# Summing 20 instead of 18 token tiles inside the expert loop, four just behind it, with tables by five stages and earlier first slots

## What is computed

```python
x = x + _L0_attn_ref(_layernorm(x), ...)   # only the first 16 tokens of each batch go through attention, three iterations
x = x + _L0_ffn_ref(_layernorm(x), ...)    # for the others attention adds a bias alone
# _L0_ffn_ref, for each token:
scores = sigmoid(tokens @ router_weight.T)      # 32 experts in 4 groups
topk_idx, topk_w = ...                          # best 2 groups, best 4 experts in them, weights normalised, times 2.5
gate_vals, up_vals = silu(tokens @ gate_w[e].T), tokens @ up_w[e].T
expert_out = (gate_vals * up_vals) @ down_w[e].T
mixed = (expert_out of the 4 chosen experts * topk_w).sum()
return mixed + shared_expert(tokens)            # a dense expert for every token
```

## Time and profile before

| | |
|---|---|
| median of 3 runs | 484.57 us (483.71 to 491.29) |
| profiled execution, its own time | 480.79 us |
| its span, first to last instruction | 478.9 us |
| PE busy | 372.5 us (78%) |
| DVE busy | 300.5 us (63%) |
| POOL busy | 298.0 us (62%) |
| ACT busy | 239.2 us (50%) |
| mean granted clock of PE | 0.927 of full speed |
| DMA | 98.01 MB, 205 GB/s over the span |

### The profile page before, as it was taken

How to read it: one execution, slowest core, us unless ns; L and a number is a source line. 1 busy time by engine, 2 the same in 40 slices (tenths; PEclk the granted TensorE clock), 3 DMA queues, 4 the chain that set the end, 5 groups by cost and what they waited for, 6 DMA issues and landing times.

```text
span 478.9 us, 9278 instructions
## 1 busy us (share of the span) xinstructions
PE 372.5 (78%) x2363; PEld 302.2 (63%) x2363; DVE 300.5 (63%) x1010; ACT 239.2 (50%) x611; POOL 298.0 (62%) x437
## 2 busy tenths in 40 slices
PE   0668989997888673479999999999999788969000
PEld 0544757573455251468899999999999677967000
DVE  3878877759988342147588854444444676858197
ACT  1546755585735552344565665666566444435000
POOL 5410888888888888688776766666666445446100
PEclk9999988999999899589999999999999989889655
DMA  7980123522386387648987755555556887687696
GB/s 173 282 257 2 60 105 108 190 106 111 113 330 235 113 331 258 230 148 272 303 273 230 228 172 157 180 167 174 167 158 208 275 287 220 214 292 225 224 407 200
DMA packets 46457, 98.01 MB, mean 205 GB/s; under 512 B 8633, under 2 KB 30782, under 8 KB 44992
## 3 DMA queue, kind: packets, MB, share of 16 engines
q1 hardware_dynamic: 33392, 62.70, 41.9%
q0 software_dynamic: 12720, 34.62, 19.4%
q10 hardware_dynamic: 288, 0.03, 0.0%
HBM read 53.93 MB, written 44.57 MB: 206 GB/s over the span
## 4 chain that ended last, share of the span: by engine, by line
PE 15%; issue 14%; POOL 13%; DVE 8%; DMA 8%; DVEq 1%; SPq 0%; ACT 0%; POOLq 0%; ACTq 0%
POOL pairs_dram L714 11%; PE two_banks L1127 8%; DVE x_sb L1731 6%; PE two_banks L1140 4%; DMA pairs_dram<-routing,loopb 2%; PE two_banks L1114 2%; DMA routing<-pairs_dram 2%; DMA loopb<-pairs_dram 2%; POOL slots_dram L706 1%; DVE staged_w L1757 1%; DMA gu_w<-pairs_dram 1%; DMA slots_dram<-loopb,slot_i 1%; DVEq L1748 1%; DVE routing L1717 1%; PE two_banks L963 0%
## 5 line engine op out<-in xcount | busy, mean ns | idle before, releaser
L714 POOL DMA_INDIRECT pairs_dram<-routing,loopb x137 | 139.3, 1017 | 85.7 <-issue 60.0
L1127 PE MATMUL two_banks<-routing,staged_w 128*128 128x128 f32 x1096 | 150.7, 282 | 2.7 <-ACT routing L855 1.7
L706 POOL DMA_INDIRECT slots_dram<-loopb,slot_i x128 | 128.1, 1001 | 27.0 <-issue 26.0
L1127 PEld LDWEIGHTS two_banks<-routing,staged_w 128*128 128x128 f32 x1096 | 138.6, 198 | 3.6 <-ACT routing L855 2.1
L1140 PE MATMUL two_banks<-dn_w,routing 128*128 x274 | 85.3, 394 | 15.1 <-DVE routing L1717 15.1
L1717 DVE TENSOR_TENSOR routing<-routing,two_banks 128x128 f32<-128x128 f32 x137 | 38.9, 284 | 76.2 <-ACT routing L860 72.5
L1757 DVE COPY staged_w<-gu_w 128x512 f32 x137 | 65.2, 476 | 16.8 <-issue 8.4
L865 ACT ACTIVATE routing<-two_banks 128x256 f32<-128x256 f32 x137 | 52.5, 383 | 38.3 <-PE two_banks L1140 38.3
L860 ACT ACTIVATE routing<-two_banks 128x128 f32<-128x128 f32 x137 | 37.9, 277 | 66.7 <-PE two_banks L1127 66.5
L954 PE MATMUL two_banks<-gu_w,sgu_w 128*128 128x512 f32 (+1 forms) x128 | 64.7, 639 | 6.8 <-DVE loopb L1513 5.8
L1114 PE MATMUL two_banks<-ident,loopb 128*128 128x128 f32 x274 | 54.3, 282 | 10.8 <-DMA loopb<-slots_dram 10.5
(11 more groups left out here) (278 smaller groups left out, 405.5 us busy)
## 6 DMA issues: line engine op xcount, KB each, us to landing
loopb<-slots_dram SPq DMA_DIRECT2D x137, 128.5 KB, 2.7
gu_w<-pairs_dram SPq DMA_DIRECT2D x14, 512.0 KB, 9.0
routing<-pairs_dram SPq DMA_DIRECT2D x12, 512.0 KB, 4.5
slots_dram<-blank SPq DMA_DIRECT2D x33, 136.0 KB, 28.1
gu_w<-in_gate_up SPq DMA_DIRECT2D x2, 2048.0 KB, 11.1
loopb<-pairs_dram SPq DMA_DIRECT2D x6, 512.0 KB, 3.9
gu_w<-in_gate_up SPq DMA_DIRECT2D x1, 2560.0 KB, 9.5
pairs_dram<-routing,loopb POOLq DMA_INDIRECT x137, 3.4
```

What stands on the lines that cost most here:

```text
L706: pool.indirect_dma_start(out=slots_dram, out_offset=bass.IndirectOffsetOnAxis(ap=slot_i[:, at:at + 1], axis=0), in_=xg[:, r, :] if n < TT ...
L714: pool.indirect_dma_start(out=pairs_dram, out_offset=bass.IndirectOffsetOnAxis(ap=xg[:, place_of(u), D:ROW].bitcast(I32), axis=0), in_=yb[ ...
L1127: ins = pe.matmul(bank[2 + u % 2][:, m * P:(m + 1) * P], staged_w[:, u % 2, c, m * I:(m + 1) * I], xT[:, u % 2, c, :], start=(c == 0), sto ...
```

## The change

Stages are now five, at tiles 8, 16, 20, 24 and 32 (`DONE_BY` 63, 95, 111, 127), in both tables. Twenty tiles are summed in the loop in pairs that start at units 72, 78, 84, 90, 104, 109, 114, 119, 124 and 129, four units each. SP issues the two loads of a pair together, at unit start + 6 of its own order. Four more tiles (q 20 to 23) are loaded when unit 126 has been scattered and summed directly behind the loop; 8 are left for the end. The first group of 8 tiles is stored in SP's unit 110. The first table has 64 entries to work on instead of 32, the second 160 instead of 96. In the first stretch the ranks and slots of tiles 1 to 8 stand earlier on PE and DVE, and the root of tiles 17 to 24 moves on POOL behind the first six indirect DMAs. ACT's program is the same.

```diff
-OUT_GROUPS = [(1, 9), (9, 17), (17, 19), (0, 1), (19, 25), (25, 28), (28, 30), (30, 32)]
-LOADS = TT - 18
+OUT_GROUPS = [(1, 9), (9, 17), (17, 21), (21, 25), (0, 1), (25, 28), (28, 30), (30, 32)]
+LOADS = TT - 24
...
-STAGES = [16, 24, TT]
+STAGES = [8, 16, 20, 24, TT]
 DONE_BY = [(TOPK * P * t + E * (P - 1)) // P for t in STAGES[:-1]]
-IN_LOOP = 18
-SUM_FROM = 101
-SUM_ORDER = [*range(1, IN_LOOP + 1), 0, *range(IN_LOOP + 1, TT)]
+SUM_AT = [72, 78, 84, 90, 104, 109, 114, 119, 124, 129]
+IN_LOOP = 2 * len(SUM_AT)
+BEFORE_END = 24
+SUM_ORDER = [*range(1, BEFORE_END + 1), 0, *range(BEFORE_END + 1, TT)]
 EARLY_LOADS = 5
-assert STAGES[0] == PARTS[1][1] - 1 and DONE_BY[-1] < FIXED and SUM_FROM + IN_LOOP * TOPK // 2 <= FIXED
+LOAD_AT = [at + 6 for at in SUM_AT]
+assert STAGES[:2] == [PARTS[0][1] - 1, PARTS[1][1] - 1] and STAGES[3] == BEFORE_END and DONE_BY[3] < FIXED
+assert all(at - RING + 1 >= DONE_BY[[2 * pair + 2 <= t for t in STAGES].index(True)] for pair, at in enumerate(LOAD_AT))
+assert SUM_AT[-1] + TOPK <= FIXED and LOAD_AT[-1] < FIXED
...
 FILL_PE = [
-    "T0 L0 T1 T2 T3 T4 L1 T5 L2 T6 L3 L4 T7 L5 L6 L7 T8 G0 T9 T10 U0 L8 L9",
-    "T11 G1 T12 X0 T13 T14 L10 U1 T15 L11 L12 L13 L14 L15 D0 T16 T17 G2 T18 U2",
+    "T0 L0 T1 T2 T3 T4 L1 T5 L2 T6 L3 L4 T7 L5 L6 L7 T8 G0 X0 T9 T10 U0 L8 L9",
+    "T11 G1 T12 T13 T14 L10 U1 T15 L11 L12 L13 L14 L15 D0 T16 T17 G2 T18 U2",
...
 FILL_DVE = [
-    "R0 R0 N6 R0 R0 R0 R0 P0 P1 P2 N0 R0 R0 U0 N1 U1",
+    "R0 R0 N6 R0 R0 R0 R0 P0 P1 P2 R0 R0 N0 U0 N1 U1",
...
             def load_rows(q):
 
                 if q == 0:
-                    sp.wait_ge(hid_ready, SUM_FROM - EARLY)
+                    sp.wait_ge(hid_ready, 14 + 2 * (3 * TOPK + 2) + 1)
                     sp.wait_ge(pair_added, SHARED + 1)
-                if q < IN_LOOP:
+                if q < BEFORE_END:
                     if q >= EARLY_LOADS:
...
-                q, rest = divmod(u - DONE_BY[0] - RING + 1, 2)
-                if q >= 0 and rest == 0:
-                    load_rows(q)
-
-            loaded = (FIXED - DONE_BY[0] - RING) // 2 + 1
-            for q in range(loaded, STAGES[0]):
+                if u in LOAD_AT:
+                    load_rows(2 * LOAD_AT.index(u))
+                    load_rows(2 * LOAD_AT.index(u) + 1)
+                if u == LOAD_AT[4]:
+                    sp.wait_ge(tile_summed, 8)
+                    store(*OUT_GROUPS[0])
+
+            sp.wait_ge(tile_summed, 16)
+            store(*OUT_GROUPS[1])
+            for k in range(OUTS):
+                sp.wait_ge(scattered[k], 16 * len(range(k, DONE_BY[3], OUTS)))
+            for q in range(IN_LOOP, BEFORE_END):
                 load_rows(q)
-            store(*OUT_GROUPS[0])
-            for k in range(OUTS):
-                sp.wait_ge(scattered[k], 16 * len(range(k, DONE_BY[1], OUTS)))
-            for q in range(STAGES[0], IN_LOOP):
-                load_rows(q)
-            sp.wait_ge(tile_summed, OUT_GROUPS[1][1] - 1)
-            store(*OUT_GROUPS[1])
...
-            for q in range(IN_LOOP, TT):
+            for q in range(BEFORE_END, TT):
                 load_rows(q)
-            for a, b in OUT_GROUPS[2:]:
+            for a, b in OUT_GROUPS[3:]:
...
-            for what in ROOTS[3:]:
+            for what in ROOTS[3:-1]:
                 inverse_root(what)
...
+                    if (n, k) == (1, 2):
+                        inverse_root(ROOTS[-1])
...
+                    if part == 1:
+                        pe.matmul(early_totals_ps[:, 0:E], ones_b[:, :], prefix[part][:, :, 0], start=True, stop=True,
+                                  skip_group_check=True)
+                        ins = pe.matmul(early_totals_ps[:, E:], ones_b[:, :], prefix[part][:, :, b - a], start=True, stop=True,
+                                        skip_group_check=True)
+                    elif part:
+                        pe.matmul(total_ps, ones_b[:, :], prefix[part][:, :, b - a], start=True, stop=True, skip_group_check=True)
+                        for k in (2, 3):
+                            ins = pe.matmul(mid_totals_ps[:, (k - 2) * E:(k - 1) * E], ones_b[:, :],
+                                            prefix[part][:, :, STAGES[k] + 1 - a], start=True, stop=True, skip_group_check=True)
...
             def early_counts():
 
-                dve.tensor_copy(e_row[:, 7, :], early_total_ps)
-                seq(dve.tensor_copy(number, early_total_ps))
-                seq(dve.tensor_scalar(number, number, 7, None, ALU.logical_shift_right))
-                seq(dve.tensor_copy(counts, number))
+                seq(dve.tensor_copy(counted[:, 0:2 * E], early_totals_ps))
+                dve.tensor_scalar(early_number[:, 0:E], counted[:, 0:E], float(P - 1), None, ALU.add)
+                seq(dve.tensor_copy(early_number[:, E:], counted[:, E:2 * E]))
+                seq(dve.tensor_scalar(early_number, early_number, 7, None, ALU.logical_shift_right))
+                seq(dve.tensor_copy(early_edges[:, E:], early_number))
+                seq(dve.tensor_tensor(early_edges[:, E:2 * E], early_edges[:, E:2 * E], early_edges[:, 2 * E:], ALU.min))
 
             def early_table():
...
+                dve.memset(before[:, 0:1], 0.0)
+                seq(dve.tensor_tensor(early_n, early_edges[:, E:], early_edges[:, 0:2 * E], ALU.subtract))
+                scan(early_ends, early_n, 2 * E)
+                seq(dve.scalar_tensor_tensor(early_step, early_edges[:, 1:2 * E + 1], float(CAP_TILES), early_edges[:, E:],
+                                             ALU.add, ALU.subtract))
...
+            def pass_late(c):
+
+                seq(dve.tensor_scalar(late_passed, late_ends, iota_u[:, c:c + 1], -float(EARLY), ALU.subtract, ALU.is_le))
+                seq(dve.tensor_reduce(ecol[:, 4 + c:5 + c], late_passed, AX.X, ALU.add))
+                seq(dve.tensor_tensor(late_passed, late_passed, late_step, ALU.mult))
+                seq(dve.tensor_reduce(ecol[:, 6 + c:7 + c], late_passed, AX.X, ALU.add))
...
-                    elif SUM_FROM <= u < SUM_FROM + IN_LOOP * TOPK // 2:
-                        pair, k = divmod(u - SUM_FROM, TOPK)
-                        for q in (2 * pair, 2 * pair + 1):
-                            add_rows(q, k)
+                    for pair, at in enumerate(SUM_AT):
+                        if at <= u < at + TOPK:
+                            for q in (2 * pair, 2 * pair + 1):
+                                add_rows(q, u - at)
```

More of the change, by code:

```diff
@@ L937, in rank @@
                                     stop=True, skip_group_check=True)
-                    if part:
-                        ins = pe.matmul(early_total_ps if part == 1 else total_ps, ones_b[:, :], prefix[part][:, :, b - a],
-                                        start=True, stop=True, skip_group_check=True)
-                    if part == len(PARTS) - 1:
-                        ins = pe.matmul(mid_total_ps, ones_b[:, :], prefix[part][:, :, STAGES[1] + 1 - a], start=True,
-                                        stop=True, skip_group_check=True)
+                    if part == 1:
[8 more added lines that the diff above has]
+                                            prefix[part][:, :, STAGES[k] + 1 - a], start=True, stop=True, skip_group_check=True)
                 else:
@@ L1344, in know_next @@
             def know_next():
-                dve.tensor_copy(e_row[:, 8, :], mid_total_ps)
+                dve.tensor_copy(counted[:, 2 * E:4 * E], mid_totals_ps)
                 seq(dve.tensor_tensor(next_slot[:, :], total_ps, first_slot[:, :], ALU.add))
-            total, number, counts, ends, step = (e_row[:, k, :] for k in range(5))
-            number = number.bitcast(I32)
-            before, taken = chunk[:, 0, :], chunk[:, 1, :]
-            def passed_by_early():
-                passed, steps = e_row[:, 5, :], e_row[:, 6, :]
-                seq(dve.tensor_tensor(passed, ends, iota_u[:, 0:1].to_broadcast([P, E]), ALU.is_le))
-                seq(dve.tensor_tensor(steps, passed, step, ALU.mult))
-                dve.tensor_reduce(ecol[:, 4:5], passed, AX.X, ALU.add)
-                seq(dve.tensor_reduce(ecol[:, 6:7], steps, AX.X, ALU.add))
-                seq(dve.tensor_scalar(ecol[:, 0:1], ecol[:, 4:5], float(E - 1), None, ALU.min))
@@ L1362, in early_counts, with rows_of @@
[L1362 to L1376 removed]
+            def rows_of(k, n):
+                return e_row[:, k:k + n, :].rearrange("p k e -> p (k e)")
@@ new lines, in _, with scan @@
+            total, L = e_row[:, 0, :], len(STAGES) * E
+            counted = rows_of(1, len(STAGES))
+            taken = chunk[:, 1, :]
+            spare = small[:, :, :].rearrange("p a n -> p (a n)")
+            early_edges = rows_of(6, 3)
+            early_number = early_edges[:, E:].bitcast(I32)
+            early_n, early_ends, early_step, early_passed = (spare[:, 2 * E * k:2 * E * (k + 1)] for k in range(4))
+            before = spare[:, 8 * E:10 * E + 1]
+            def scan(ends, n, width):
```

(7 more changed lines are left out.)

68 lines of the change are left out of this document (31 added, 37 removed).

## The result

The changed kernel takes **462.3 us** (median of 4 runs, 459.5 to 463.4) beside 484.66 for the kernel before: ratio **0.956**, 95% interval 0.952 to 0.960. Forecast: 459, range 449 to 470. Its profiled execution took 463.41 us with a span of 461.6; the one before had 478.9.

A forecast was written before the change was run, and what follows sets the result against it. Bounds taken: PE in the plain loop, DVE's waits for late rows in the sums, DVE at the end, POOL's moves before the loop. 480.8 - 17.8 - 9.5 + 1.7 + 2.0 = 457.2, plus 2: 459 us, range 449 to 470.

The forecast's parts named there:

- Loop: Loads and sums in the expert loop: DVE's waits for pair rows should go, gaining 17.8 us, bounds 18.4 or nothing.
- the room: In the loop, time between a pair's second load landing and DVE wanting it: 3.2 us, where before it was none.
- Rivals 1 and 5: In the loop: rows still late, 473 us (0.13); or slower, every pair waits, about 505 us (0.03).
- rival 1: In the loop: scatters or paired loads land later and eat the 3.2 us of room, 473 us; chance 0.13.
- End: Behind the loop: fourteen tiles become eight, so 24 additions fewer on DVE, 9.5 us gained.
- DVE stays the bound: At the end: the 8 loads left arrive faster (1.3 us) than DVE takes for a tile (1.6 us).
- They lie inside the 8.79 us: Directly behind the loop: four tiles' additions, 6.4 us, fit while DVE waits 8.79 us for the first late load.
- First stretch: At the start: POOL's earlier moves against a later root, with DVE taken 4 us late, a loss of 1.7 us.
- covered by ACT's 10.75 us: Before the loop: the later attention costs nothing because ACT waits 10.75 us at tile 28; without cover 4 us.
- rival 2: At the start: DVE's 4.8 us lost in full, first tile loads late, table costs 3; 463 us, chance 0.10.
- Tables: First table: about 2 us of DVE in the attention, under cover; second, units 4 to 7: 2.0 us, bounds 0 and 3.
- rival 4: In the loop: eight more additions held by POOL's scatters, 7.7 us, giving 467 us; chance 0.02.

The follow-up runs named there:

- e6: The changed kernel with the loads of each pair three units later in SP's order (last pair one unit); median 475.67 us, ratio 0.974.
- e10: The kernel before with 16 tiles summed in the loop instead of 18, from unit 105 instead of 101, loads where they were; median 468.41 us, ratio 0.972.
- e12: The changed kernel run again, unedited, on another chip; median 462.51 us, ratio 0.957 to the kernel before.
- e4: The changed kernel with the root of tiles 17 to 24 behind the first three indirect DMAs instead of six; median 459.49 us, ratio 0.945.
- e8: The changed kernel with the 512 KB store of tiles 17 to 20 moved behind the last eight loads in SP's order; median 462.75 us.
- e11: The changed kernel with the four tiles behind the loop loaded and summed with the others at the end; median 463.9 us, ratio 0.962.
- e1: The changed kernel with its first stretch in the old order, stages, loads and sums still changed; median 458.17 us, ratio 0.947.
- e7: e1 with the first table's work on DVE moved from step 20 of the attention to step 8; median 458.1 us.
- e5: The kernel before with 20 unused additions ahead of the first table's work in the attention on DVE; median 492.87 us, ratio 1.012.

## Why the prediction was right, and where it was not

- **Loop, right.** -17.8 forecast; from unit 20 to 136 it is 431.77 - 251.37 = 180.4 us instead of 197.9, so -17.5. e6 takes the room away and most of the loss is back (12.5 us); e10 gives room (and two tiles fewer) and the loss is gone. Rivals 1 and 5 did not happen, but the changed kernel is near rival 1: DVE waited 2.4, 2.1 and 1.2 us for rows in the loop of e12, e4 and e8. The room was smaller than stated: 6.7 + 2 x 0.4 + 4.7 + 1.3 is 13.5 us and not 13.1, so 2.8 us were left of 16.3, not 3.2.
- **End, mis-sized.** -9.5 forecast, -6.4 measured. The 24 additions went as computed. The step that failed is "DVE stays the bound": the first late load came 11.4 us behind the last product instead of 9.9, and DVE stood 2.27 us for the second one instead of 0.79. That is 3.1 us, and e8 and e11, with one trace each, point to its source: I costed four loads and a store ahead of the last scatter at nothing. "They lie inside the 8.79 us" was true of DVE and not of the DMA engines.
- **First stretch, mis-sized: the cover was not there.** Forecast +1.7, with 4 us of DVE lateness under the cover of ACT's 10.75 us at tile 28. DVE was late as I said (4.22 us for the root, `shift` at 54.59 for 55.5). POOL lost its lead, but earlier than I said: at 78.46 us, waiting for ACT's staging, and only then at the slots. "They are what the start of the loop waits for", said of the moves, is right as far as a move's landing ends last. The step that failed is "covered by ACT's 10.75 us": beside ACT's wait PE stood 10.51 us for a tile load that hangs on the table behind the attention, so the cover was the 1.73 us that PE then still stood for ACT. And the moves themselves come late with the attention, for POOL waits for ACT's staging inside it. So the whole lateness arrives at unit 0. e1 gives the order +4.0 us by the trace and 4.1 by medians: about the 4 that I took off. This is what rival 2 said of DVE's lateness and of the first tile loads (it had 0.10); its 3 us for the table did not come.
- **Tables, half right.** +2.0 for the second: units 0 to 20 took 43.4 us instead of 43.1, so it cost 0.35; by the medians of all traces with the second table changed and unchanged, 43.6 and 42.8, it cost 0.8. The first had been given 2 us under the same cover; it takes 1.2 us more in the attention by the trace of e1 (147.33 to 150.83, before 147.37 to 149.71). e7 could not show it apart from the start's own variation.
- **The sum, in part luck.** -23.6 forecast between profiled executions, -17.4 measured: 0.3 us missing in the loop, 3.1 at the end, 2.9 in the start with the tables, 6.2 together. That the median is only 3.3 us above the forecast is luck for the rest: I added 2 us to come from a profiled execution to the median, and the median of the changed kernel lies 1.1 us under its profiled execution. The profile of before was early, 3.9 us under its median: e10 has the same first stretch and starts unit 0 5.2 us later. I gave the stops for rows as the reason for such differences. The runs do not bear it out: those of e10, almost without such stops, lie 6.1 us apart, and those of e5, with them, 3.6.
- **Additions beside scatters.** In the loop an addition now takes 0.475 and 0.477 us in the mean (48 and 32 of them), and at the end, where POOL has nothing more to issue, 0.480 (the last 32). The loop's pace leaves no room for the 7.7 us of rival 4. By the rule of the Trainium skill (GPSIMD Engine Reference, Specifications) that POOL and VectorE contend for SBUF when VectorE has two inputs there, they should be longer beside scatters; the trace does not show it.

## What to carry to other kernels

A long wait of an engine is cover only as far as nothing else that the next work needs is late with it. Ask which wait ends second and how far behind it the last one ends: here ACT waited 10.75 us and the cover was 1.73. Several runs with fixed distances show it better than one (from the staging of tile 28 to unit 0 it was 4.35 us in twelve of fourteen). A wait that a load causes is taken away by distance between issue and use, not by fewer bytes: give each load the landing that the chain shows plus a few us, and check what stores stand in front of it (in e12 a store of 1 MB did and DVE waited 2.4 us for rows, though that store alone was not tried). Work put into an idle engine's time is free only if its transfers do not run beside the transfer that the next stage waits for.
